# Cross-attention and expert MLP: the next batch's softmax shift made two tiles early and seeded into all its tiles, with GpSimd adding tiles 1 to 4 of the sums

## The reference

```python
x = x + xattn(layernorm(x), ctx, mask, Wq, Wkv, Wout, bout)
# in xattn, per batch and head
dots = einsum('bhnd,bhmd->bhnm', q, k) * SCALE
dots = dots - (1.0 - mask)[:, None, :, None] * MASK_NEG
attn = softmax(dots, axis=-1)
out = einsum('bhnm,bhmd->bhnd', attn, v) ... @ Wout + bout
# then, with expert b for batch b
x = x + gelu(layernorm(x) @ w1[b] + b1[b]) @ w2[b] + b2[b]
```

## Time and profile before

| | |
|---|---|
| median of 3 runs | 416.08 us (415.92 to 416.37) |
| profiled execution, its own time | 416.03 us |
| its span | 414.2 us |
| PE busy | 396.8 us (96%) |
| DVE busy | 302.4 us (73%) |
| ACT busy | 206.2 us (50%) |
| POOL busy | 57.6 us (14%) |
| mean granted TensorE clock | 0.989 |

### The profile page before, as it was taken

The page is one execution under the profiler, slowest core; times in us unless marked ns, Lnnn a source line. Parts: engine busy times, 40 slices in busy tenths (PEclk is TensorE's granted clock), DMA queues, the critical chain, the costliest instruction groups (busy, mean ns, idle before and its releaser), DMA issues.

```text
span 414.2 us, 5556 instructions
## 1 busy us (share of the span) xinstructions
PE 396.8 (96%) x1721; PEld 286.6 (69%) x1721; DVE 302.4 (73%) x490; ACT 206.2 (50%) x274; POOL 57.6 (14%) x47
## 2 busy tenths in 40 slices
PE   8499899999999999999999999999999999999995
PEld 7376577766776677757775877757676877677685
DVE  5278866987788768968896689887888688266343
ACT  3144635366545635375547355465456354655421
POOL 0411240150015000420042000600060000000000
PEclk9789999999999999999999999999999999999998
DMA  6760002014001400025004100044002000300000
GB/s 212 216 222 14 2 0 74 2 38 110 1 2 41 109 0 3 0 77 178 0 0 111 38 0 0 5 113 136 0 8 66 0 0 10 97 2 0 3 2 3
DMA packets 20661, 19.62 MB, mean 47 GB/s; under 512 B 904, under 2 KB 17576, under 8 KB 20648
## 3 DMA queue, kind: packets, MB, share of 16 engines
q1 hardware_dynamic: 20648, 19.45, 15.4%
HBM read 19.21 MB, written 0.23 MB: 47 GB/s over the span
## 4 chain that ended last, share of the span: by engine, by line
PE 88%; DVE 4%; SPq 3%; issue 1%; ACT 1%; DMA 1%; ACTq 0%; DVEq 0%
PE ps_a L411 34%; PE ps_s L386 27%; PE ps_x L419 10%; PE ps_x L438 4%; PE ps_x L426 3%; SPq L294 2%; PE ps_a L361 2%; PE ps_x L458 2%; PE ps_x L467 2%; PE ps_s L397 2%; PE ps_x L334 1%; DVE log_sum L779 1%; DMA bout_sb<-in_b_out 1%; ACT inv_sum L621 1%; PE ps_s L513 1%
## 5 line engine op out<-in xcount | busy, mean ns | idle before, releaser
L411 PE MATMUL ps_a<-ex,ctx_sb 125*128 125x448 f32 x384 | 172.2, 541 | 0.0
L591 ACT ACTIVATE ex<-ps_s 125x896 f32<-125x896 f32 x96 | 88.1, 917 | 121.0 <-PE ps_s L386 93.2
L751 DVE TENSOR_REDUCE chunk_max<-ps_x 128x1 f32<-128x500 f32 x168 | 111.3, 675 | 32.8 <-PE ps_x L419 29.4
L419 PE MATMUL ps_x<-ctxt_hi,qk_hi 128*128 128x500 f32 x168 | 90.1, 538 | 10.7 <-DVE inv_sum L860 5.8
L411 PEld LDWEIGHTS ps_a<-ex,ctx_sb 125*128 125x128 f32 x384 | 71.3, 189 | 27.6 <-issue 21.6
L748 DVE TENSOR_TENSOR ex_sum<-ex_sum,ex 125x896 f32<-125x896 f32 x80 | 86.7, 1083 | 4.6 <-ACT ex L591 4.6
L386 PE MATMUL ps_s<-qk_hi,ctxt_hi 128*125 128x448 f32 x192 | 87.4, 536 | 0.0
L598 ACT COPY ps_s<-shift_row 125x896 f32<-125x896 f32 x80 | 72.9, 911 | 10.0 <-DVE shift_row L868 7.9
L386 PEld LDWEIGHTS ps_s<-qk_hi,ctxt_hi 128*125 128x125 f32 x192 | 35.8, 187 | 35.7 <-issue 35.1
L386 PE MATMUL ps_s<-qk_hi,ctxt_lo 128*125 128x448 f32 x192 | 57.2, 379 | 0.0
L994 POOL TENSOR_TENSOR qk_lo<-qk,qk_hi 128x448 fp32r<-128x448 f32 x16 | 23.7, 1483 | 225.8 <-DVE qk_hi L772 216.7
(11 more groups left out here) (79 smaller groups left out, 262.9 us busy)
## 6 DMA issues: line engine op xcount, KB each, us to landing
ctxt_raw<-in_ctx_t SPq DMA_DIRECT2D x8, 750.0 KB, 7.6
ctx_sb<-in_ctx SPq DMA_DIRECT2D x8, 750.0 KB
w_sb<-in_w SPq DMA_DIRECT2D x4, 512.0 KB, 3.8
w_sb<-in_w SPq DMA_DIRECT2D x8, 256.0 KB, 4.3
ex<-in_wq_t SPq DMA_DIRECT2D x2, 256.0 KB, 4.0
ex<-in_wk_t SPq DMA_DIRECT2D x2, 256.0 KB, 4.5
att_n<-in_wv_t SPq DMA_DIRECT2D x1, 512.0 KB, 4.3
att_n<-in_w_out SPq DMA_DIRECT2D x1, 512.0 KB, 5.8
```

The costliest lines, as they stand in the source:

```text
L411: mm = nc.tensor.matmul(ps_a[:, c, 0:CH], ctx_sb[0:MT, u, t, :], ex[0:MT, t % RING, c * CH:(c + 1) * CH], start=(t == 0), stop=(t == TM - 1))
L419: nc.tensor.matmul(bank[:, 0:MC], qk_hi[:, u, t * P:(t + 1) * P], ctxt_hi[:, u, k * MC:(k + 1) * MC], start=True, stop=True).then_inc(job_ ...
L591: nc.scalar.activation(half(ex[0:MT, slot, :]), src, ACT.Exp, scale=SCALE).then_inc(ex_ready, 1)
L751: nc.vector.tensor_reduce(chunk_max[:, k, t:t + 1], filled()[:, 0:MC], AX.X, ALU.max).then_inc(job_free, 1)
```

## The change

It does four things.

- **Shift early.** The 21 maxima end at (9, 2), one table for all batches. `shifts` moves to (9, 3), the two shift jobs and their copies to `shift_row` (now double) move to (10, 2) of the iteration before.
- **All tiles seeded.** Tiles 0 and 1 of batches 1 to 7 are seeded by ScalarE, in tiles 10 and 11 of the iteration before; their four matmuls of line 397 go. Batch 0 keeps them.
- **GpSimd adds tiles 1 to 4** to `ex_sum`; VectorE adds 5 to 11 and waits for GpSimd's fourth.
- Semaphores and counts follow (`ex_summed_first`, `ex_summed_last`).

```diff
+    MAX_AT = [(1, 1), (1, 2), (2, 0), (2, 1), (2, 2), (3, 2), (4, 0), (4, 1), (4, 2), (5, 0), (5, 1),
+              (6, 0), (6, 1), (6, 2), (7, 0), (7, 1), (8, 0), (8, 2), (9, 0), (9, 1), (9, 2)]
...
-    SHIFT_AT = (0, 1)
-    SEEDED = TM - 2
+    FIRST_SHIFT_AT, SHIFTS_AT, SHIFT_AT = (0, 1), (9, 3), (10, 2)
+    POOL_SUMS = 4
+    DVE_SUMS = TM - 1 - POOL_SUMS
...
             # TensorE, scores
-                seed = t >= 2
+                seed = t >= 2 or b.i is not None or b.off > 0
...
             # TensorE, jobs_at
-                    if at == SHIFT_AT:
+                    if (b.off == 0 and at == FIRST_SHIFT_AT) or (prepare and at == SHIFT_AT):
+                        if at == SHIFT_AT:
+                            pe.wait_ge(shift_ready, b.later(1).at(1, 1))
                         for c in range(2):
                             shift_rows(job()[:, 0:CH], P, c, start=True).then_inc(job_ready, 1)
...
             # ScalarE, seed
-                if t == 2:
+                if t == (2 if b.i is None and b.off == 0 else 0):
                     act.wait_ge(job_free, jobs.value())
-                nc.scalar.copy(ps_s[0:MT, t % 2, :, 0:CH], half(shift_row[0:MT, :])).then_inc(seeded, 1)
+                nc.scalar.copy(ps_s[0:MT, t % 2, :, 0:CH], half(shift_row[0:MT, b.parity, :])).then_inc(seeded, 1)
...
             # ScalarE, iteration
                     if t + 2 < TM:
                         seed(b, t + 2)
+                    elif prepare:
+                        seed(b.later(1), t + 2 - TM)
...
             # VectorE, iteration
-                    if prepare and at == (TM - 1, 1):
+                    if prepare and at == SHIFTS_AT:
                         shifts(b.later(1))
...
-                    if t > 1:
+                    if t - 1 > POOL_SUMS:
                         add_tile(b, t - 1)
...
             # GpSimd
+            def add_tile(b, t):
+
+                pool.wait_ge(ex_ready, b.at(TM, t + 1))
+                dst = ex_sum[0:MT, b.parity, :]
+                left = ex[0:MT, 0, :] if t == 1 else dst
+                if t > 1:
+                    pool.wait_ge(ex_summed_first, b.at(POOL_SUMS, t - 1))
+                nc.gpsimd.tensor_tensor(dst, left, ex[0:MT, t % RING, :], ALU.add).then_inc(ex_summed_first, 1)
...
                 for t in range(TM):
+                    if 1 <= t <= POOL_SUMS:
+                        add_tile(b, t)
```

More of the change, by code:

```diff
@@ L140, in xattn_ffn @@
     FOLD_AT = [(3, 0), (3, 1), (3, 2), (4, 0)]
-    SHIFT_AT = (0, 1)
-    SEEDED = TM - 2
-    assert all(len(m) == QT * KM and SHIFT_AT < m[0] for m in MAX_AT)
-    FIRST_JOBS = 2 + 2 * QT * KM + 2 + 4
+    FIRST_SHIFT_AT, SHIFTS_AT, SHIFT_AT = (0, 1), (9, 3), (10, 2)
+    POOL_SUMS = 4
+    DVE_SUMS = TM - 1 - POOL_SUMS
+    assert len(MAX_AT) == QT * KM and FIRST_SHIFT_AT < MAX_AT[0] and MAX_AT[-1] < SHIFTS_AT < SHIFT_AT < OUT_AT
+    FIRST_JOBS = 2 + QT * KM + 2 + 4 + QT * KM + 2
     ROUND_JOBS = 2 * (QT * KM + 2 + 2) + 4
@@ L167, in xattn_ffn @@
         shift_diag = sb("shift_diag", [P, QT, P], F32R)
-        shift_row = sb("shift_row", [P, Q])
+        shift_row = sb("shift_row", [P, 2, Q])
         chunk_max = sb("chunk_max", [P, KM, QT])
@@ L311, in _ @@
             load_experts(ROUNDS)
-            for e, drained in enumerate((2 + 2 + 4, 2 + 2 + 4 + 2 + 4)):
+            for e, drained in enumerate((2 + 4, 2 + 4 + 2 + 4)):
                 sp.wait_ge(job_free, FIRST_JOBS + ROUNDS * ROUND_JOBS + drained)
@@ L652, in iteration @@
                 for t in range(TM):
-                    if t == 0:
+                    if t == 0 and b.off == 0:
                         jobs.n += 2
                     if t == SUM_AT[0] and b.off > 0:
-                        jobs.n += sum(at < SUM_AT for at in MAX_AT[b.parity]) if prepare else 0
+                        jobs.n += sum(at < SUM_AT for at in MAX_AT) if prepare else 0
                         inverse_sums(b.later(-1))
-                        jobs.n += sum(at > SUM_AT for at in MAX_AT[b.parity]) if prepare else 0
-                        jobs.n += 4 if pair is not None else 0
+                        jobs.n += sum(at > SUM_AT for at in MAX_AT) if prepare else 0
+                        jobs.n += 3 if pair is not None else 0
                     if pair is not None:
@@ L669, in iteration @@
                         att_out(b.later(-1))
+                    if t == SHIFT_AT[0] and prepare:
+                        jobs.n += 2 + (4 + len(MAX_AT) if b.off == 0 else 0)
                     if t + 2 < TM:
                         seed(b, t + 2)
+                    elif prepare:
+                        seed(b.later(1), t + 2 - TM)
+                    if t == TM - 1 and pair is not None:
+                        jobs.n += 1
             def drain_fold(n):
@@ L704, in _ @@
             iteration(Batch(None, 0))
-            jobs.n = FIRST_JOBS
+            assert jobs.n == FIRST_JOBS
             with act.Fori(0, ROUNDS) as i:
@@ L744, in add_tile @@
                 dst = ex_sum[0:MT, b.parity, :]
-                left = ex[0:MT, 0, :] if t == 1 else dst
-                if t > 1:
-                    dve.wait_ge(ex_summed, b.at(TM - 1, t - 1))
-                nc.vector.tensor_tensor(dst, left, ex[0:MT, t % RING, :], ALU.add).then_inc(ex_summed, 1)
+                if t == POOL_SUMS + 1:
+                    dve.wait_ge(ex_summed_first, b.at(POOL_SUMS, POOL_SUMS))
+                else:
+                    dve.wait_ge(ex_summed_last, b.at(DVE_SUMS, t - 1 - POOL_SUMS))
+                nc.vector.tensor_tensor(dst, dst, ex[0:MT, t % RING, :], ALU.add).then_inc(ex_summed_last, 1)
             def max_part(k, t):
@@ L864, in drain @@
                 def drain(at):
-                    if at == SHIFT_AT:
-                        wait(dve, seeded, b.at(SEEDED, 0))
+                    if (b.off == 0 and at == FIRST_SHIFT_AT) or (prepare and at == SHIFT_AT):
+                        u = b.parity if at == FIRST_SHIFT_AT else 1 - b.parity
+                        wait(dve, seeded, b.at(TM, -2))
                         for c in range(2):
-                            nc.vector.tensor_copy(shift_row[:, c * CH:(c + 1) * CH], filled()[:, 0:CH]).then_inc(job_free, 1)
+                            nc.vector.tensor_copy(shift_row[:, u, c * CH:(c + 1) * CH], filled()[:, 0:CH]).then_inc(job_free, 1)
                     if b.off == 0 and at in FOLD_AT:
```

26 lines of the change are left out of this document (14 added, 12 removed), and 4 rows, old and new, of the table MAX_AT.

## The result

| | before | changed |
|---|---|---|
| median, same chip | 416.27 us (415.92 to 416.7) | 430.96 us (430.13 to 432.25) |
| ratio | | 1.0356, 95% interval 1.0334 to 1.0377 |
| profiled execution | 416.03 us | 431.92 us, span 430.1 |

The change costs 14.7 us. Forecast were 427.1 and a range up to 431.0, so the time lies 3.9 us above the number, at the range's upper edge. The sign came out; one term of the sum was 1.8 us too small and two were missing.

The account below looks back on a forecast made before the run. The prediction took TensorE's in-order stream to bound the kernel, busy 396.8 of 414.2 us. Its terms, -5.7 - 1.3 + 3.9 + 6.3 + 6.9 + 1.0 = +11.1 on 416.03, gave 427.1 us, range 418 to 431.

Parts of the forecast that it names:

- step 3: At (10, 2), TensorE's shift jobs wait about 0.25 us for `shift_diag`, 0.55 with refill and handover, seven times: +3.9 us.
- 1 matmuls: Tiles 0 and 1 of seven batches each lose a pair of line 397's matmuls on TensorE: -5.7 us.
- 2 batch 0: In batch 0, VectorE's casts run without GpSimd's low parts beside them, so a TensorE wait goes: -1.3 us.
- 5 refinement held: GpSimd's third add holds VectorE's refinement in tile 3; TensorE waits at (4, 2) in six iterations: +6.9 us.
- 5 normalisation held: GpSimd's fourth add meets the attention output's normalisation at (4, 3), delaying the output projection at (5, 2) four times: +1.0 us.
- Step 4: In pair iterations, ScalarE's first seed delays the gelu functions; TensorE waits at (11, 2), three times 2.1 us: +6.3 us.
- Its bound below: The gelu delay in pair iterations costs nothing if the first seed is released by 255.1.
- Step 5: GpSimd's adds, 2.2 us each, hold VectorE's two-input refinement and meet its normalisation: +6.9 and +1.0 us.
- Step 6: Loads: `ctxt_lo` and the following context load come some 17 us later, costing nothing unless a load takes over 15 us.
- The rival without holding: GpSimd's adds don't hold VectorE in tiles 3 and 4, so their cost falls away: 419.2 us, chance 0.19.
- the one of longer adds: GpSimd's adds take 2.9 us and catch more of VectorE's two-input work: 434 us, chance 0.08.
- The faster rival: VectorE's lead frees the first seed in time in pair iterations' tile 10; without holding too, 412.9 us, chance 0.11.

Follow-up runs that it names:

- the cap first: All suspected costs removed, plus VectorE's gelu cap moved ahead of its add of tile 9 in pair iterations' tile 10: 411.85 us, ratio 0.9896.
- the mended kernel: Changed kernel with adds on VectorE, first seed behind gelu, gelu product earlier, shift jobs later, batch 0's low parts held: 413.4 us, 0.9937.
- the memsets: Changed kernel with each GpSimd add replaced by a one-column add and a memset of 2240 columns: 422.25 us, ratio 1.0149.

## Why the forecast came out 3.9 us low: step 3 mis-sized, two terms left out

| term | forecast | measured | by |
|---|---|---|---|
| 1 matmuls | -5.7 | -5.7 | 28 matmuls fewer, at the price of the earlier trace rows |
| 2 batch 0 | -1.3 | -1.3 | one edit each: -1.6 and -1.2 |
| 3 `shift_diag` | +3.9 | +5.7 | 3.9 of waits, 7 x 0.26 of refills |
| 4 gelu behind the seed | +6.3 | +5.8 | 3 x 1.93 |
| 5 refinement held | +6.9 | +7.3 | 6 x (0.95 + 0.27) |
| 5 normalisation held | +1.0 | +0.9 | 3 x 0.3 |
| a maximum at (7, 1) | none | +1.3 | 3 x (0.15 + 0.27) |
| sum | +11.1 | +14.0 | 14.1 measured, clock at full |

The table counts along the changed kernel's trace. Taken alone, with the cap first, step 3 costs 3.55, since there its wait in a pair iteration covers most of a later one and the loop's first plain iteration waits 0.55 instead of 0.81.

**Step 3 is the term that was mis-sized**, 3.9 where the trace has 5.7. The mechanism held: seven waits for `shift_diag` at (10, 2). What was off is the lag between the two engines, in small pieces that all point one way. The forecast took 252.80 for the end of the maximum of (9, 2). That is where the next add begins, and an add that doesn't need the result can begin before it is there:

```profile
251.63 1.26 DVE L751 TENSOR_REDUCE chunk_max<-ps_x 128x1 f32<-128x500 f32 x2
```

The reductions ended at 252.89, so the lag was 0.48 and not 0.39. In the changed kernel they end at 166.01 (164.76 + 1.25), 0.52 behind the time that lies 1.98 ahead of TensorE's arrival at (10, 2) (168.00 - 0.53 = 167.47). The first step of `shifts`, which needs them, begins 0.03 later (166.04), `shift_diag` ends 1.83 behind that instead of 1.81 (167.87), and the matmul begins 0.13 behind it, not 0.03. 0.09 + 0.04 + 0.03 + 0.02 + 0.10 = 0.28 makes 0.53 out of 0.25, which is 254.61 - 254.39 with the handover of 0.03. The step said 0.55 with the refill, and it is 0.79.

The later plain iterations, with 0.57, are like it. In the loop's first one a small step ahead of `shift_diag` also stopped 0.31 us for the one before, so that `shift_diag` began 1.01 us behind the first reduction (118.20 - 117.19) instead of 0.74 (166.78 - 166.04): 0.81. The four kernels that have GpSimd's adds or memsets beside the early shift all show this stop, though GpSimd is idle then, and the kernels with all adds on VectorE don't (0.55 there), so the cost of 0.26 comes with GpSimd's part of the change. How is open.

**The wait at (7, 1) was not in the sum.** The kernel with all adds on VectorE keeps it, so the maxima's new order is the likely source, though no run changes the order alone. The pair iteration has three new places, (4, 1), (5, 1) and (7, 1), and the forecast followed only (4, 1).

**The clock was not in the sum either.** In the profiled execution it adds 1.6 us behind a wait of 1.9. If it is what parts the two groups of runs, it lifts the median from 430.2 to 431.

**Step 4** was right to 0.5 us: ScalarE's functions began at 171.16 behind the seed at 170.31, and with the seed behind them the wait went from 1.90 to 0.61. Its refill was put at 0.2, and none to speak of is there (0.03). Its bound below was wrong: it said that a first seed released in time makes the step nothing, but even with the seed behind both functions 0.61 stayed, from the add ahead of the product, and 0.77 in the mended kernel, from the cap behind `shift_diag` and an add.

**Step 5** was right in its two directions, its add (2.2 estimated, 2.12 to 2.17 measured) and its place. It counted the maximum at (4, 1) only as 0.23 us of TensorE's time and didn't say that without it the job at (4, 2) would need another bank. That its number came out owes something to luck: by the same reasoning I expected these waits of the adds alone too, where there are none. The normalisation costs at three output projections, not four. **Step 6** held: no wait for a load is among TensorE's in the loop. The rival without holding (419) fell with the refinement's 2.65 us; the one of longer adds (434) fell with 2.17. The faster rival fell at its own condition: the copies to `shift_row` ended at 170.28, 2.8 us behind TensorE's arrival at (10, 2), where it needed 0.7, with four adds fewer on VectorE.

The early shift itself pays once its followers are put in order: 411.6 to 411.9 us against 416.15, of which 1.2 to 1.6 is batch 0's. The 7.0 us of steps 1 and 2 are not all there: 0.6 + 0.5 us of waits in the pair iterations and their refills, some 2 us, are left.

## What to carry to other kernels

When work moves off an engine that waits in order, ask which of its instructions is late next, not how much it has to do: VectorE lost 26 us of work here, and its refinement, its normalisation and its gelu product came later. A producer moved next to its consumer needs the lag of the whole chain between them at that place, small dependent steps included, and the lag is read from where an instruction ends, not from where the next, independent one begins. Waits in series on one in-order engine cover one another, so the price of one can be read only with the others gone: the shift's later place was worth nothing in a pair iteration with the gelu late and 0.32 us with the gelu in time. In all it was worth nothing in the first case, where a fall of the clock took the plain iterations' 2.5 us, and 3.6 us in the second.

## What the runs showed of the hardware

- **The granted clock fell behind short waits.** TensorE idled 1.90 or 2.67 us in a stream that was busy before and after, and behind some of these waits, not all, its clock read 0.57 to 0.58 for four microseconds (16 matmuls in 2.55 and 2.78 us instead of 1.55), then 1.00. It was one of three waits of 1.9 in the profiled execution of the changed kernel, none of three with all adds on VectorE and none of three with the memsets, two of three of 2.67 with the shift jobs later, none at 0.61. The same wait of 1.90 with and without it stands in one trace. What decides whether it falls the runs don't show.
- **A GpSimd add of 896 columns** took 2.17 us (mean of 24) where VectorE's takes 1.08, and held a two-input VectorE instruction that came behind it for the rest of its run (1.08 to 2.65). A GpSimd subtraction of 448 columns was held in its turn by one ahead (1.13 to 1.98). A memset of 1.97 us held none.
- **A small dependent step on VectorE** (128x7) began 0.47 us behind the one before it in the loop's first plain iteration (117.53 to 118.00), where steps of this size else begin 0.20 to 0.34 behind. It did so in all four kernels with GpSimd's adds or memsets and the early shift, and in none with all adds on VectorE. Why is open.
- **Casts with one SBUF input were held too:** two took 2.62 us beside GpSimd's subtractions and 0.74 without, which cost batch 0 1.2 to 1.6 us in the kernel before.
